# A two-layer spectral filter on one core: layer 0's block stages for two steps at a time, an earlier forward H, and T in another PSUM bank

## The reference

```python
# layer 0
f  = fft2(x, axes=(1, 2), norm='ortho');  Xh = f.real - f.imag     # 23 of 90 width modes kept
o1 = relu(einsum('bhwni,nio->bhwno', Xk, w1[0]) + b1[0])           # 8 blocks of 48 channels
o2 = einsum('bhwni,nio->bhwno', o1, w2[0]) + b2[0]
x  = ifft2(softshrink(o2, LAM), s=(H, W), norm='ortho').real + x
# layer 1: the same with complex weights
xf  = rfft2(x, axes=(1, 2), norm='ortho')
o1r = relu(mm(xr, w1[0]) - mm(xi, w1[1]) + b1[0])
o1i = relu(mm(xi, w1[0]) + mm(xr, w1[1]) + b1[1])
o2r = softshrink(mm(o1r, w2[0]) - mm(o1i, w2[1]) + b2[0])
o2i = softshrink(mm(o1i, w2[0]) + mm(o1r, w2[1]) + b2[1])
y   = irfft2(o2r + 1j * o2i, s=(H, W), norm='ortho') + x
```

## Time and profile before

| | |
|---|---|
| median of 3 runs | 519.68 us (517.36 to 519.83) |
| profiled execution | 517.78 us, span of the trace 516.0 us |
| TensorE busy | 479.6 us, 93% of the span |
| VectorE, ScalarE, GpSimd busy | 308.1, 209.8, 172.5 us |
| mean granted TensorE clock | 0.975 of full |
| DMA | 105.25 MB, mean 204 GB/s |

### The profile page before, as it was taken

The page is one execution under the profiler, slowest core; times in us unless marked ns, Lnnn a source line. Parts: engine busy times, 40 slices in busy tenths (PEclk is TensorE's granted clock), DMA queues, the critical chain, the costliest instruction groups (busy, mean ns, idle before and its releaser), DMA issues.

```text
span 516.0 us, 14920 instructions
## 1 busy us (share of the span) xinstructions
PE 479.6 (93%) x6172; PEld 342.5 (66%) x6172; DVE 308.1 (60%) x674; ACT 209.8 (41%) x473; POOL 172.5 (33%) x194
## 2 busy tenths in 40 slices
PE   4679999999999999999999999999999999999763
PEld 1357787777777677767777677767777767886521
DVE  7634456457754677456764677456763577567643
ACT  0015544553355443543354433554345434444201
POOL 9821323123441244223442144312433122322134
PEclk9959999999999999999999999999999999999978
DMA  9998773677899688886989588987989665644498
GB/s 213 265 237 236 213 187 110 145 207 182 252 233 243 165 201 264 218 216 178 267 224 252 152 210 263 228 204 187 256 213 258 169 168 163 148 108 113 121 224 268
DMA packets 77416, 105.25 MB, mean 204 GB/s; under 512 B 7744, under 2 KB 63826, under 8 KB 77350
## 3 DMA queue, kind: packets, MB, share of 16 engines
q1 hardware_dynamic: 57766, 56.74, 41.4%
q0 software_dynamic: 10608, 40.66, 29.8%
q10 hardware_dynamic: 8976, 6.90, 5.7%
HBM read 52.84 MB, written 51.43 MB: 202 GB/s over the span
## 4 chain that ended last, share of the span: by engine, by line
PE 77%; DMA 7%; DVE 5%; POOL 3%; issue 2%; ACT 2%; SPq 1%; ACTq 1%; POOLq 0%
PE ps L702 13%; PE ps L636 13%; PE ps L727 12%; PE ps L689 11%; PE ps L597 10%; PE ps L649 8%; PE ps L714 5%; PE ps L665 4%; PE ps L675 3%; DMA img<-x 2%; DVE img L572 2%; DMA wt<-weights 2%; POOL xs L392 2%; DVE ns L546 2%; ACT p L463 1%
## 5 line engine op out<-in xcount | busy, mean ns | idle before, releaser
L572 DVE TENSOR_TENSOR img<-ps,img 90x768 f32<-90x768 f32 x92 | 82.6, 900 | 19.0 <-PE ps L636 15.5
L392 POOL TENSOR_TENSOR xs<-xs,nt 128x360 f32<-128x360 f32 (+1 forms) x48 | 41.6, 866 | 147.9 <-DVE nt L524 122.5
L636 PE MATMUL ps<-jr,cst 64*90 64x384 f32 (+1 forms) x358 | 80.0, 515 | 6.4 <-DVE img L572 5.7
L597 PE MATMUL ps<-img,cst 128*64 128x384 f32 (+1 forms) x368 | 70.1, 494 | 8.9 <-DMA img<-x 8.0
L401 POOL DMA_DIRECT2D y<-img x42 | 34.7, 826 | 130.7 <-DVE img L572 130.3
L456 ACT ACTIVATE o<-ps,wt 97x180 f32<-97x180 f32 (+1 forms) x96 | 33.9, 406 | 108.7 <-PE ps L689 108.7
L546 DVE SCALAR_TENSOR_TENSOR ns<-p,ps 109x384 f32<-109x384 f32 x96 | 53.1, 553 | 38.2 <-ACT p L463 33.4
L702 PE MATMUL ps<-wt,o 128*64 128x96 f32 x1472 | 74.4, 250 | 0.1
L649 PEld LDWEIGHTS ps<-cst,bt 128*64 128x64 f32 x1472 | 62.5, 140 | 16.9 <-issue 13.9
L702 PEld LDWEIGHTS ps<-wt,o 128*64 128x64 f32 x1472 | 65.4, 138 | 12.5 <-issue 12.5
L689 PE MATMUL ps<-xs,wt 64*97 64x180 f32 (+1 forms) x768 | 68.9, 317 | 3.4 <-POOL xs L392 3.2
(11 more groups left out here) (43 smaller groups left out, 410.9 us busy)
## 6 DMA issues: line engine op xcount, KB each, us to landing
y<-img POOLq DMA_DIRECT2D x35, 540.0 KB, 5.4
img<-x POOLq DMA_DIRECT2D x25, 540.0 KB, 8.6
scr_i<-et SPq DMA_DIRECT2D x48, 270.0 KB, 5.4
scr_f<-fs SPq DMA_DIRECT2D x154, 72.0 KB, 3.4
bt<-scr_f SPq DMA_DIRECT2D x40, 270.0 KB, 5.5
jr<-scr_i SPq DMA_DIRECT2D x48, 216.0 KB, 5.3
img<-x ACTq DMA_DIRECT2D x10, 576.0 KB, 7.8
y<-img SPq DMA_DIRECT2D x11, 270.0 KB, 3.7
```

What stands on the lines that cost most here:

```text
L392: nc.gpsimd.tensor_tensor(re, re, nt[s % 2][:, :, 0:kws(s), 0:H], ALU.subtract).then_inc(re_ok, 1)
L572: nc.vector.tensor_tensor(y, p, y, ALU.add).then_inc(i_add, 1)
L597: last = mm(ps[64 * r:64 * r + 64, P3 + g % 2, 0:(b - a) * HC], K["w_fwd"], img[t % IMGS][:, a:b, :].rearrange("p h c -> p (h c)"), start= ...
L636: last = mm(ps[0:W, B0 + r, 0:n], K["w_inv"][64 * r:64 * r + 64, :], set_rows(t, j)[64 * r:64 * r + 64, at, 0:n], start=True, stop=True)
```

## The change

- `c0` and `d0` run once for two steps, over the 360 columns of both (315 for positions 4 and 5). Their buffers (`xs`, `xd`, `o10`, `p0`, `nt`) hold two steps. ScalarE takes `d0`'s relu in one instruction for each half, VectorE's shrink of a half waits for its own. GpSimd subtracts for both steps, one after the other; the loads of task 2's first rows that stand behind it go out two at a time.
- `a` runs two steps ahead instead of one. `a` of s waits for the copies of `a` of s-1, and for the `e` copies one step further back. Loads are issued in the middle of the step, three steps ahead; a task's first step's load keeps its place.
- `t` writes into P2+1, the second bank of layer 1, and no longer waits for `d0_ss`; `c1` of s waits for the additions of `t` of s-1. `t` comes right behind `a`, in front of the second two forward W groups. At position 4 (`late_h`) the order after `d0` is inverse group, `t`, `a`.
- The refill of a task's last image chunk is an entry of its own in the list, at the same place.

The diff, cut to its core:

```diff
+def late_h(s):
+    return s < NSTEPS and s % STEPS == STEPS - 2
...
-    order += [("load", 0), ("load", 1), ("a", 0), ("x", 0)]
+    order += [("load", 0), ("load", 1), ("load", 2), ("a", 0), ("a", 1), ("x", 0)]
...
-        if s + 2 < NSTEPS:
+        t_ = [("t", s - 1)] if 0 < s <= NSTEPS else []
+        a_ = [("a", s + 2)] if s + 2 < NSTEPS else []
+        if s + 2 < NSTEPS and (s + 2) % STEPS == 0:
             order.append(("load", s + 2))
+        if i == 1 and t > 1:
+            order.append(("refill", t - 2, NXC - 1))
         if 0 < s <= NSTEPS:
             order.append(("c1", s - 1))
         order += inv[s][0:1]
         if s > 1:
             order.append(("e", s - 2))
         order += inv[s][1:2]
-        if s < NSTEPS:
-            order.append(("c0", s))
+        if s + 3 < NSTEPS and (s + 3) % STEPS != 0:
+            order.append(("load", s + 3))
+        if s < NSTEPS and s % 2 == 0:
+            order.append(("c0", s // 2))
         if 0 < s <= NSTEPS:
             order.append(("d1", s - 1))
-        if s < NSTEPS:
-            order.append(("d0", s))
+        if s < NSTEPS and s % 2 == 0:
+            order.append(("d0", s // 2))
         if s < 3:
             order.append(("x", 2 * s + 1))
+        if late_h(s):
+            order += inv[s][2:3] + t_ + a_
+            continue
         order += fwd[s][0:2]
-        if s + 1 < NSTEPS:
-            order.append(("a", s + 1))
+        order += a_ + t_
         if i == 1 and 0 < t < TASKS:
             order += [("rows", t - 1, j) for j in range(JR)]
         order += fwd[s][2:4]
         if s < 2:
             order.append(("x", 2 * s + 2))
-        if 0 < s <= NSTEPS:
-            order.append(("t", s - 1))
         order += inv[s][2:3]
...
-                    nc.scalar.activation(p0[:, :, 0:kws(s) * H], ps[:, P1:P1 + 2, 0:kws(s) * H], ACT.Relu).then_inc(d0_p, 1)
+                    for q in range(2):
+                        nc.scalar.activation(p0[:, q, 0:n], ps[:, P1 + q, 0:n], ACT.Relu).then_inc(d0_p, 1)
...
                 if kind == "a":
                     s, = what
-                    if s >= 3:
-                        pe.wait_ge(e_act, s - 2)
-                        pe.wait_ge(e_dve, s - 2)
+                    if s > 0:
+                        pe.wait_ge(a_act, s)
+                        pe.wait_ge(a_dve, s)
+                    if s >= 4:
+                        pe.wait_ge(e_act, s - 3)
+                        pe.wait_ge(e_dve, s - 3)
...
-                    pe.wait_ge(xd_ok, s + 1)
-                    if s > 0:
-                        pe.wait_ge(d0_ss, 2 * s)
-                    if s > 1:
-                        pe.wait_ge(t_add, 2 * s - 2)
+                    pe.wait_ge(xd_ok, 2 * j + 2)
+                    if j > 0:
+                        pe.wait_ge(d0_ss, 2 * j)
...
                     if s > 0:
                         pe.wait_ge(d1_ss, 2 * s)
+                        pe.wait_ge(t_add, 2 * s)
...
                 if kind == "t":
                     s, = what
                     pe.wait_ge(d1_ss, 2 * s + 2)
-                    if s + 1 < NT:
-                        pe.wait_ge(d0_ss, 2 * s + 4)
...
-                            last = nc.tensor.transpose(ps[0:rows, P1, 256 * p + 128 * q:256 * p + 128 * q + 128],
+                            last = nc.tensor.transpose(ps[0:rows, P2 + 1, 256 * p + 128 * q:256 * p + 128 * q + 128],
...
                 if kind == "e":
                     s, = what
-                    if s + 2 < NT:
-                        pe.wait_ge(a_act, s + 3)
-                        pe.wait_ge(a_dve, s + 3)
+                    pe.wait_ge(a_act, min(s + 4, NT))
+                    pe.wait_ge(a_dve, min(s + 4, NT))
```

More of the change, by code:

```diff
@@ L25 @@
 NSTEPS = TASKS * STEPS
+PAIR = 2 * STEP
 GROUPS = -(-H // 4)
@@ L181, in spectral_layers @@
         bt = [sb(f"bt{k}", [128, STEP * HC + 16]) for k in range(BT)]
-        xs = [sb(f"xs{k}", [128, 2, STEP, 2 * H]) for k in range(2)]
-        xd = sb("xd", [128, 2, STEP * H])
-        o10 = sb("o10", [128, 2, STEP * H])
-        p0 = sb("p0", [128, 2, STEP * H])
+        xs = [sb(f"xs{k}", [128, 2, PAIR, 2 * H]) for k in range(2)]
+        xd = sb("xd", [128, 2, PAIR * H])
+        o10 = sb("o10", [128, 2, PAIR * H])
+        p0 = sb("p0", [128, 2, PAIR * H])
         ev = sb("ev", [128, 2, H])
-        nt = [sb(f"nt{k}", [128, 2, STEP, 64]) for k in range(2)]
+        nt = [sb(f"nt{k}", [128, 2, PAIR, 64]) for k in range(2)]
         o11 = sb("o11", [128, 4, STEP, 64])
@@ L383, in _ @@
                     pool.wait_ge(a_dve, s + 1)
-                    xt = xs[s % 2][:, :, 0:kws(s), :]
-                    nc.gpsimd.tensor_tensor(xd[:, :, 0:kws(s) * H].rearrange("p q (k m) -> p q k m", m=H), xt[:, :, :, 0:H], xt[:, :, :, H:2 * H],
+                    n, k = of_step(s)
+                    xt = xs[n][:, :, k, :]
+                    nc.gpsimd.tensor_tensor(xd.rearrange("p q (k m) -> p q k m", m=H)[:, :, k, :], xt[:, :, :, 0:H], xt[:, :, :, H:2 * H],
                                             ALU.subtract).then_inc(xd_ok, 1)
                 if kind == "d0":
-                    s, = what
-                    pool.wait_ge(d0_ss, 2 * s + 2)
-                    pool.wait_ge(d0_sym, 2 * (s // STEPS + 1))
-                    re = xs[s % 2][:, :, 0:kws(s), 0:H]
-                    nc.gpsimd.tensor_tensor(re, re, nt[s % 2][:, :, 0:kws(s), 0:H], ALU.subtract).then_inc(re_ok, 1)
-                    if s < NXC:
-                        r0, r1 = s * XCH, min(s * XCH + XCH, H)
-                        pool.dma_start(img[2][0:WPAD, r0:r1, :], first_rows(1, 0, s)).then_inc(x_ld[2][s], 16)
+                    j, = what
+                    pool.wait_ge(d0_ss, 2 * j + 2)
+                    pool.wait_ge(d0_sym, 2 * (2 * j // STEPS + 1))
+                    for s in (2 * j, 2 * j + 1):
+                        n, k = of_step(s)
+                        re = xs[n][:, :, k, 0:H]
+                        nc.gpsimd.tensor_tensor(re, re, nt[n][:, :, k, 0:H], ALU.subtract).then_inc(re_ok, 1)
+                    for c in (2 * j, 2 * j + 1):
+                        if c < NXC:
+                            r0, r1 = c * XCH, min(c * XCH + XCH, H)
+                            pool.dma_start(img[2][0:WPAD, r0:r1, :], first_rows(1, 0, c)).then_inc(x_ld[2][c], 16)
                 if kind == "inv" and what[0] < TASKS - 1 and (what[1] % 2 == 1 or what[1] == GROUPS - 1):
@@ L409, in _ @@
                     nc.gpsimd.tensor_tensor(y, p1[0:W], y, ALU.add).then_inc(i_pool, 1)
-                if kind == "load" and what[0] % STEPS == 3 and what[0] // STEPS >= 2:
-                    refill(what[0] // STEPS - 2, NXC - 1)
+                if kind == "refill":
+                    refill(*what)
             for t in range(TASKS - IMGS, TASKS - 1):
@@ L515, in _ @@
                 if kind == "d0":
-                    s, = what
-                    n, t0, even = kws(s), nt[s % 2], s % STEPS == 0
-                    dve.wait_ge(d0_p, s + 1)
+                    j, = what
+                    t0 = nt[j % 2]
+                    even, n = 2 * j % STEPS == 0, pair_cols(j)
+                    k0 = int(even)
                     for q in range(2):
+                        dve.wait_ge(d0_p, 2 * j + q + 1)
                         if even:
@@ L553, in _ @@
                         v = ns[0:rows, p, :, 0, :]
-                        nc.vector.tensor_tensor(v, ps[0:rows, P1, 256 * p:256 * p + 256].rearrange("p (n c) -> p n c", c=64)[:, :, 0:BS], v, ALU.add).then_inc(t_add, 1)
+                        nc.vector.tensor_tensor(v, ps[0:rows, P2 + 1, 256 * p:256 * p + 256].rearrange("p (n c) -> p n c", c=64)[:, :, 0:BS], v, ALU.add).then_inc(t_add, 1)
                 if kind == "e":
@@ L667, in _ @@
                 if kind == "d0":
-                    s, = what
-                    n, f = kws(s) * H, s // STEPS % HALVES
-                    pe.wait_ge(c0_act, s + 1)
-                    pe.wait_ge(c0_dve, s + 1)
+                    j, = what
+                    n, f = pair_cols(j), 2 * j // STEPS % HALVES
+                    pe.wait_ge(c0_act, j + 1)
+                    pe.wait_ge(c0_dve, j + 1)
                     for q in range(2):
@@ L713, in _ @@
                         for q in range(2):
-                            last = nc.tensor.transpose(ps[0:rows, P1, 256 * p + 128 * q:256 * p + 128 * q + 128],
-                                                       nt[s % 2][:, q, 2 * p:2 * p + kw, :].rearrange("p k m -> p (k m)")[:, 0:rows], K["ident"])
+                            last = nc.tensor.transpose(ps[0:rows, P2 + 1, 256 * p + 128 * q:256 * p + 128 * q + 128],
+                                                       nt[at][:, q, kk.start + 2 * p:kk.start + 2 * p + kw, :].rearrange("p k m -> p (k m)")[:, 0:rows], K["ident"])
                     last.then_inc(t_mm, 1)
```

56 lines of the change are left out of this document (33 added, 23 removed).

## The result

| | before | after |
|---|---|---|
| median of 4 runs each, on one chip | 519.75 us (517.36 to 520.12) | 525.94 us (522.88 to 530.06) |
| ratio, after to before | | 1.0152, interval 1.0111 to 1.0194 |
| profiled execution | 517.78 us, span 516.0 | 526.32 us, span 524.5 |

The change makes the kernel slower by 1.5%, by the ratio on record; the quotient of the two medians is 1.0119. The forecast was 525.2 us and "slower"; the median came out 0.7 us above it. From profile to profile the forecast was +7.4 us, and +8.5 was measured. As will be seen, two of its terms were too high or too low by 2 us and one was missing, and they nearly cancelled. That the sum is better than its parts is luck.

The account below looks back on a forecast made before the run. TensorE, busy 336.12 of 340 us mid-kernel, was taken as the bound, its 8.2 us saving used up by switching and waits. 517.78 + 1.0 (middle tasks) + 1.7 (last) + 4.75 (first) = 525.2 us, range 516 to 533.

Parts of the forecast that it names:

- The bound, and TensorE's 8.2 us: TensorE bounds the middle; joining c0 and d0 blocks over 24 pairs saves 0.17 us per block, 8.2 us less.
- Positions 0, 1, 2, 4 and 5: Steps by place in a middle task: +1.02, -1.0, +0.7, +0.8 and -0.94 us.
- Position 3: Middle task: -0.42 us; T ahead of W adds its 0.57, as the inverse still cannot come earlier.
- Queues: SyncE's loads and POOL's subtracts, store and refill: counted as nothing, up to 1 us as bound for position 4's load.
- The last task: No W covers T, and chains from d0 to c1 show: +1.7 us, bounds +0.8 to +2.6.
- The start: First task: second H and c0 wait, partly at half clock; next c1 +3.4 us, between +0.3 and +7.
- The early load at position 4 of the first task: H of task 1 moves up and waits for its load: +1.85 us from d0 to c1, including 0.22.
- "faster" rival: New waits in the middle and last tasks are not paid: 514.5 us; chance 0.13.
- "same" rival: The start costs little, with the clock back early (+0.3) and T at 0.44: 519.4 us; chance 0.17.
- Loads late: Loads take over 10.5 us and each late one costs TensorE its lateness: 536 us; chance 0.08.
- That a two-step block might cost as much as two: A 360-column block costs 0.93 us, two old ones: 533.4 us; chance 0.04.

Follow-up runs that it names:

- Experiment 1: Changed kernel with each product of the joined c0 and d0 cut into two of 180 columns, same block; blocks 0.77 us, span 2.5 us shorter.
- Experiment 4: Changed kernel with the inverse's row loads at position 1 moved behind the second W pair's stores; 522.03 us, ratio 1.0068 to the kernel before.
- experiment 5: Unused products fill the start's idle places in the changed kernel and the kernel before; first forward H to c1 of step 1 takes 19.46 and 17.39 us.
- experiments 2: Changed kernel with T back behind the second forward W pair at positions 1 to 3, new bank kept; middle task +0.77 us, span +2.2 us.
- experiment 8: Changed kernel with d1 and an inverse group ahead of d0, inverse H behind, at positions 0, 4 (last task also 2); span 6.8 us less.
- experiment 6: Changed kernel with the last task's held inverse groups set around T; last task and end together 87.93 us against 89.52.

## Why the prediction was right, point by point

**The bound, and TensorE's 8.2 us: right.** Blocks of 0.77 and 0.69 as worked out from the earlier trace rows (0.46 + 4 x 0.075 is 0.76, by a hundredth less than the sum has it; the rows gave 0.76 and 0.77). Experiment 1 shows that the saving is a fixed cost of the block, not of the instruction.

**Positions 0, 1, 2, 4 and 5: right to 0.2 us.** The chains came out as added up, within 0.03 us at position 0. The 0.19 by which the whole of position 0 was too high is a wait ahead of it: before the change the first inverse group there waited 0.22 us for VectorE, and that is gone, which the forecast did not count. At position 4 a part of it is luck: the sum took H at full length, 1.39, on both sides. Before the change H has 24 records there, and a wait of 0.23 for VectorE's shrink behind it made up the 1.38 from its start to T's.

**Position 3: the mechanism right, its size off in both directions.** Without late stores it is -0.62, not -0.42, mainly because the forward H there has 24 records, not 32, and takes 1.03 us, where the sum had taken H's full length: with H two steps ahead, that of the step of 3 width modes falls on position 3, and no longer on 4. With them it is up to +0.98. The failed step is in "Queues": SyncE was looked at for the loads only, and found harmless; its stores, and ScalarE's buffers that hang on them, were not followed. Experiment 4 shows them at 3.9 us in one profile, and 0.8% in the ratios (1.0152 against 1.0068), 0.5% in the quotients of the medians (1.0119 against 1.0069).

**The last task: right** (+1.71 against +1.7), with `c1` waiting 0.81 for the additions at positions 1, 2, 3 and 5, and 1.25 for GpSimd at 4.

**The start: mis-sized, +1.4 instead of +3.4.** The chain was right in kind and costs 2.07 at equal clock; what was wrong was to let the low clock last longer than before. It was low for 10.24 us instead of 13.65 and cost 0.7 less. The bounds +0.3 to +7 held it in this execution. The other seven profiles with the same start (experiment 5) lie 1.1 us under to 0.8 over the 20.36 of the kernel before: the clock, which the prediction named as what would make it wrong above all, decides this, and it differs between executions.

**The early load at position 4 of the first task: mis-sized.** H waits 0.41 for it, not 1.1; the position is +1.24, not +1.85. (In the other profiles with this order, this position takes 8.13 to 8.95 us where it took 8.62 here.)

**The end: not foreseen.** Nothing in the forecast touched the stretch behind the last `c1`; it took 1.9 us more, with a stretch of low clock that this kernel shows in some executions and not in others.

So 2.75 us too much in the first task stand against 2.0 too little in the middle and 1.9 missing at the end; that they nearly cancelled is luck. The "faster" rival fell with experiments 2 and 8: the waits are paid, and even where filled they come back in part as shape changes. The "same" rival needed the clock back early and T at 0.44; the clock did come back earlier, in the other executions more so, but T took 0.62. "Loads late" did not happen in the changed kernel (one load took 10.3 us and landed 0.58 us before its use), but twice in kernels that were a little quicker. That a two-step block might cost as much as two is out by the rows above.

## What to carry to other kernels

When TensorE is busy 99% of a stretch, joining two blocks saves the fixed part of one of them, and this is easy to read from two widths of the same block. What it costs is read from the other engines: follow each chain from the last product that feeds it to the first that waits for it, and fill that distance with TensorE work of the same tile shape. Then follow every queue past which an entry moves, stores and their buffers too, not only the loads. And before a difference of 1 or 2 us is explained from two profiles, see how far profiles of the same order differ there: here the start, the late stores and the stretch behind the last `c1` each moved by 2 us and more.

## What the runs showed of the hardware

- A block of four products in 64x64 quadrants takes 0.77 us with 8 records of 360 columns and with 16 of 180 (experiment 1): a fixed 0.17 us belongs to the block. An inverse group takes 0.69 us ahead of `e`, which has its tile shape, and 0.81 ahead of `d0`, which has not (experiment 8).
- The granted clock of one and the same kernel averaged 0.56 in a stretch of 3.4 us in one execution and stayed at 1.00 in another, with TensorE busy throughout that stretch in both (experiment 6). In eight profiles with the same start it was at 0.50 there for 0 to 10.24 us (experiment 5).
- Stores that were ready but stood in SyncE's queue behind six loads came out 4.1 us late (158.0 to 162.13): the first load waited until 158.5, and the six took 3.57 us to issue. It cost TensorE time only ten us later, through ScalarE's buffers (experiment 4).
